# Another order of t's, s's and h's weight preparation, ahead of the loop and in its first step

## What is computed

```
kx = modulated_linear(x, cond, k...)        # 512 x 512 weights, scaled per batch by a style
A  = softmax(scores of the 16 heads of a token among themselves)   # 16 x 16 per token
x  = x + modulated_linear(A @ kx, cond, o...)

h = ln(ln(x, pw[path]), cp[comp]);  t = ln(x, tm[time]);  s = ln(x, ms[scale])
m, n, r = x + a row per batch
cat = [w0*h, w1*t, w2*m, w3*n, w4*r, w5*s]                # 6 x 512 wide
x = x + ln(silu(cat @ W1 + b1) @ W2 + b2, g, b)
```

## Time and profile before

| | us |
|---|---|
| median of three runs | 855.19 |
| lowest, highest | 854.5, 855.64 |
| the profiled execution | 856.02 |
| its span in the trace | 854.2 |

### The profile page before, as it was taken

How to read it: one execution, slowest core, us unless ns; L and a number is a source line. 1 busy time by engine, 2 the same in 40 slices (tenths; PEclk the granted TensorE clock), 3 DMA queues, 4 the chain that set the end, 5 groups by cost and what they waited for, 6 DMA issues and landing times.

```text
span 854.2 us, 19739 instructions
## 1 busy us (share of the span) xinstructions
PE 818.0 (96%) x7482; PEld 684.3 (80%) x7482; DVE 652.6 (76%) x1077; ACT 497.5 (58%) x853; POOL 588.1 (69%) x763
## 2 busy tenths in 40 slices
PE   5996888999999999999999999999999999999996
PEld 5853766888888888888888888888888888888885
DVE  3589797779887878779888778779887877778652
ACT  3595646465756647465756647565756647564531
POOL 2279659767777766777777766767777766756462
PEclk9899899999999999999999999999999999999998
DMA  8973243435544342435444342425444342333210
GB/s 279 418 259 85 63 93 75 118 66 151 107 135 113 87 106 64 118 66 152 106 138 111 87 107 62 119 67 151 108 117 104 87 110 60 106 69 82 50 51 26
DMA packets 104366, 95.56 MB, mean 112 GB/s; under 512 B 72880, under 2 KB 78160, under 8 KB 102608
## 3 DMA queue, kind: packets, MB, share of 16 engines
q1 hardware_dynamic: 95056, 69.26, 30.9%
q0 software_dynamic: 4608, 16.78, 7.2%
q10 hardware_dynamic: 4608, 8.25, 2.9%
HBM read 69.60 MB, written 8.40 MB: 91 GB/s over the span
## 4 chain that ended last, share of the span: by engine, by line
PE 84%; DVE 5%; POOL 3%; ACT 3%; DMA 2%; issue 2%; ACTq 1%; SPq 0%; DVEq 0%; POOLq 0%
PE acc L414 39%; PE tok L414 29%; PE att L414 8%; PE xp L567 6%; PE xp L414 3%; DMA kb<-in_kb 1%; POOL raw_t L1778 1%; DVE stg_e L1345 1%; POOL Wol L1701 1%; DMA BD<-q 0%; ACT junk L979 0%; ACT BD L956 0%; DVE W1sl L1336 0%; DVE W1hl L1336 0%; SPq L311 0%
## 5 line engine op out<-in xcount | busy, mean ns | idle before, releaser
L1772 POOL TENSOR_TENSOR op1l<-ytmp,op1h 128x512 f16<-128x512 f32 x64 | 81.1, 1266 | 29.0 <-ACT op1h L932 28.6
L1719 POOL TENSOR_TENSOR xlo<-xraw,xhi 128x512 fp32r<-128x512 f32 x31 | 40.7, 1313 | 56.2 <-ACT xhi L822 56.1
L414 PE MATMUL acc<-op0h,W1xh 128*128 128x256 f32 x256 | 76.1, 297 | 1.2 <-DVE op0l L1437 1.2
L414 PE MATMUL acc<-op0l,W1xh 128*128 128x256 f32 x256 | 72.4, 283 | 0.0
L414 PE MATMUL acc<-op0h,W1xl 128*128 128x256 f32 x256 | 72.3, 282 | 0.0
L414 PE MATMUL acc<-op1h,W1th 128*128 128x256 f16 x256 | 69.8, 273 | 0.0
L414 PE MATMUL acc<-op2h,W1sh 128*128 128x256 f16 x256 | 69.8, 273 | 0.0
L414 PE MATMUL acc<-op1l,W1th 128*128 128x256 f16 x256 | 69.8, 273 | 0.0
L414 PE MATMUL acc<-op1h,W1tl 128*128 128x256 f16 x256 | 69.8, 273 | 0.0
L414 PE MATMUL acc<-op2l,W1sh 128*128 128x256 f16 x256 | 69.8, 273 | 0.0
L414 PE MATMUL acc<-op2h,W1sl 128*128 128x256 f16 x256 | 69.8, 273 | 0.0
(11 more groups left out here) (287 smaller groups left out, 2815.3 us busy)
## 6 DMA issues: line engine op xcount, KB each, us to landing
xsq<-in_x SPq DMA_DIRECT2D x32, 256.0 KB, 3.1
xb<-in_x SPq DMA_DIRECT2D x32, 256.0 KB, 3.1
out<-xb SPq DMA_DIRECT2D x32, 256.0 KB, 2.3
BD<-q SPq DMA_DIRECT2D x124, 64.0 KB, 2.1
BD<-v SPq DMA_DIRECT2D x124, 64.0 KB, 3.5
xraw<-in_xT SPq DMA_DIRECT2D x30, 256.0 KB, 3.0
ring<-in_k_wT ACTq DMA_DIRECT2D x6, 256.0 KB, 3.5
dmb<-dm_rows SPq DMA_DIRECT2D x6, 256.0 KB, 4.0
```

The lines of the kernel that those rows point to most:

```text
L414: return e.matmul(o, a, b, start=start, stop=True, skip_group_check=True)
L1719: e.tensor_tensor(xlo[:, :, :], (xraw1 if g == 1 else xraw)[:, :, :], xhi[:, :, :].bitcast(F32), ALU.subtract).then_inc(s["xlo"], 1)
L1772: e.tensor_tensor(op_of[n]["l"][:, :, half(g)], four(ytmp[YT[n, g][0]]), op_of[n]["h"][:, :, half(g)], ALU.subtract).then_inc(s[f"o{n}l"], 1)
```

## The change

On GpSimd, scaled("t") moves from behind scales() to behind bounds(3), add_ob(1) moves up into its old place, and lo_16("t") moves behind gather(1) and is parted by true_scale(2). On ScalarE, z_copy(0) moves ahead of the two waits, scaled_hi("s") ahead of u_make(0), split_hi of t behind x1_hi(0), and scaled_hi("h") behind exponential(2). On VectorE, low_16("s") moves in the first step from ahead of product(pa, "h") to behind it. The numbers that are waited for on s["wh"] follow the new order (s is 1, x 2 to 5, t 6). Every instruction is still there, and the work in the steps behind the first is the same.

```diff
--- before.py
+++ after.py
@@ -1063,18 +1063,17 @@
             split_x(3)
             a_hi(1)
             squares(3)
+            z_copy(0)
             e.wait_ge(s["m2"], 3)
-            e.wait_ge(s["nst"], 8)
-            split_hi(W1["t", "h"], raw["t"], s["wh"])
-            z_copy(0)
+            scaled_hi("s")
             u_make(0)
             score_low(2)
             for kt in range(4):
                 e.wait_ge(s["xc"], kt + 3)
                 e.copy(W1["x", "h"][:, kt, :], stg["e"][:, kt, :]).then_inc(s["wh"], 1)
             x1_hi(0)
-            scaled_hi("s")
-            scaled_hi("h")
+            e.wait_ge(s["nst"], 8)
+            split_hi(W1["t", "h"], raw["t"], s["wh"])
             x1_hi(1)
             prod_hi(0, "t")
             z_make(1)
@@ -1082,6 +1081,7 @@
             e.wait_ge(s["pa"], 1)
             e.activation(t2[:, 0:256].bitcast(BF16), rp[:, :], ACT.Copy, scale=up).then_inc(s["tp"], 1)
             exponential(2)
+            scaled_hi("h")
             for k in range(1, NT + 1):
                 a, b, pa, pb = 2 * k, 2 * k + 1, 2 * k - 2, 2 * k - 1
                 front, more = k < NT, k < NT - 1
@@ -1331,7 +1331,7 @@
 
             def low_16(n, kts):
 
-                e.wait_ge(s["wh"], 6 if n == "s" else 7)
+                e.wait_ge(s["wh"], 1 if n == "s" else 7)
                 for kt in kts:
                     i = e.scalar_tensor_tensor(out=W1[n, "l"][:, kt, :], in0=raw[n][:, kt, :], scalar=beta, in1=W1[n, "h"][:, kt, :], op0=ALU.mult, op1=ALU.subtract)
                 i.then_inc(s["wlx"], 1)
@@ -1597,9 +1597,9 @@
                 product(pb, "s")
                 if front and not mod:
                     one_hot(k)
+                product(pa, "h")
                 if k == 1:
                     low_16("s", range(4))
-                product(pa, "h")
                 if mod and mod[1] == 0:
                     mod_lo(*mod, (2, 3))
                 if front:
@@ -1832,20 +1832,20 @@
             inverse_norms()
             true_scale(1)
             scales()
-            scaled("t")
+            add_ob(1)
             root1(0)
             affine(0)
             x_lo(3)
             bounds(3)
-            add_ob(1)
+            scaled("t")
             root2(0)
             add_ob(2)
-            e.wait_ge(s["wh"], 1)
-            e.wait_ge(s["Pm"], 3)
-            lo_16("t", s["wlp"])
             root1(1)
             gather(1)
+            e.wait_ge(s["wh"], 6)
+            lo_16("t", None, (0, 1))
             true_scale(2)
+            lo_16("t", s["wlp"], (2, 3))
             e.wait_ge(s["dmW"], 16)
             prod_lo(0, "t")
             for k in range(1, NT + 1):
```

## The result

| | before | after |
|---|---|---|
| median, us (runs) | 854.68 (20) | 857.07 (20) |
| lowest to highest, us | 853.06 to 857.05 | 854.24 to 859.06 |
| the profiled execution, us (its span) | 856.02 (854.2) | 858.63 (856.8) |

The ratio is 1.0023, with a 95% interval of 1.0014 to 1.0033: 2.0 us slower (1.2 to 2.8). The median before is 0.5 us under that of the three runs known ahead, so 1.9 us forecast stand against 2.0 by the ratio and 2.4 by the medians. The forecast of 857.1 met the median of 857.07, and part of that is luck: the term for x_T(1) was 1.3 us too large, and about as much more is in the runs than the traces show for any term.

A forecast was written before the change was run, and what follows sets the result against it. TensorE was taken as the bound behind the first step, VectorE's run as setting values(3); +2.7 - 0.3 - 0.6 + 0.1 = +1.9 us gave a median forecast of 857.1 us, 8-in-10 range 854.3 to 859.4.

The forecast's parts named there:

- the term for x_T(1): TensorE's x_T(1) in the first step: starts at 92.0, 2.7 us later than before, ends 1.7 and 3.5.
- The bound: Behind the first step TensorE's own work sets the end; shifts where it passes 141.53 us count one for one.
- the first part: t's scaling behind the fourth bound on GpSimd: u_make(0) 3.3 us later, x_T(1) 2.7 us later.
- the faster rival: VectorE's run to values(3) gets shorter as its 120.22 instruction meets GpSimd in another phase: -1.2 us, 854.0; chance 0.15.
- VectorE waits out the GpSimd instruction under way: VectorE instructions with two SBUF operands wait for GpSimd's to end; one x_weights of some 5 us beside the scaling.
- ScalarE's order: ScalarE's s high part is free in the wait for root2(0); h's is covered by the wait ahead of z_copy(1).
- "nothing" for t's low part: GpSimd's t low part, with true_scale(2) between, ready near 100, TensorE asking near 105: no cost.
- 0.5 for h: scaled_hi("h") ahead of z_copy(1) on ScalarE: takes back at most 0.5 us if TensorE's clock recovers sooner.
- Low part of s: VectorE's low_16("s") behind product(0,"h"): -0.6 us on the run to values(3); TensorE's 2.99 us wait moves later.
- The clock: TensorE's low clock: -0.3 us behind x_T(1) (0 to -0.8), +0.1 behind values(3) (0 to +1.3).
- The sum: All terms up to 141.53 us on TensorE: +2.7 - 0.3 - 0.6 + 0.1 = +1.9 us.
- theory C: For second traces: x_T(1) to z_T(1) on TensorE usually near 7 us before, near 8.2 with late u, by clock recovery.

The follow-up runs named there:

- With the clock kept up: The changed kernel with nine extra matmuls ahead of u_T(0) and ten ahead of x_T(1) on TensorE; 856.41 us, ratio 1.0008 to the kernel before.
- the halves: The changed kernel with scaled("t") cut in two: two kt behind scales(), two behind root2(0); 852.38 us, ratio 0.9970 to the kernel before.
- the kernel before, filled: The kernel before with ten extra matmuls, results overwritten later, in TensorE's 3.5 us wait ahead of x_T(1); 854.84 us, ratio 0.9996.

## Why the prediction was right, and where it was not

**The bound.** Right as far as the traces can tell: TensorE is as full behind scores(4) as it was, and the rest of the span varies by up to 1.9 us between traces without going with the change.

**x_T(1) later by 2.7 us: the direction was right, the size was not.** It was 1.4 (27.09 and 27.06 us behind L1797, before 25.63 twice), just under the low end of 1.7. The working has four sizes in it, and the first part is the term that was mis-sized. The bound ended 1.3 us sooner, where I counted 0.95. The scaling took 5.7 us (5.8 forecast). root2(0) took 1.7 us, not 2.2; most of the x_weights had passed by then, since the scaling held only the first of them, and not to its end. And u_make(0) to x_T(1) took 5.86 us, not 6.2, since add_ob(2) held up nothing. u_make(0) was thus 2.4 us late instead of 3.3. Two readings were off without moving this: the shortest of the four x_low ran behind lo_16("t"), not beside it, and the 1.2 us of the faster rival add up to 1.1 with its own 0.6 for product(0,"h").

**VectorE waits out the GpSimd instruction under way.** This was the step that failed in part. In all five traces with the scaling whole between bounds(3) and root2(0) the first x_weights(2) took 3.39 to 3.40 us and ended 1.2 us before the scaling did; with root2(0) ahead the last one took 4.04 us and ended 1.2 us before it too. The prediction had one x_weights of some 5 us, to the scaling's end. The lock that the Trainium skill describes ("SBUF — State Buffer", section "SBUF: two separate sides") holds for the whole instruction; here there was a wait of 2.7 us, but not to the end. On this point the measurement decides.

**ScalarE's order, and "nothing" for t's low part.** Moving h alone costs nothing that can be told. With the clock kept up a 1.12 us wait appears at values(2), as it does with the halves (1.13); the kernel before, filled, has 0.23. I had allowed 0.5 for h. But VectorE's e is 1.17 us later behind z_T(1) than in the filled kernel before, and 0.70 of that is there when the exponential starts, ahead of h: it waits for true_scale(2), for which the prediction put nothing. Only the other 0.47 us can be h's. No run moved true_scale(2) alone.

**Low part of s.** Right: -0.6 us in three pairs of traces, -1.0 by the runs (0.1 to 2.0). TensorE's 2.99 us wait went and came back at z_T(2) and values(3), as VectorE's bound demands.

**The clock: right in the traces, open in the runs.** The low clock of the first step was read too long: the granted clock is still 1.00 from 114.9 to 115.4 us and 0.50 only from 116 on, so 4.1 us should be about 3.5. I took -0.3 us up to z_T(1) and +0.1 behind values(3). In the two pairs of traces the two stretches sum to -0.1 and -0.2 us (8.22 + 8.28 against 8.38 + 8.23; 7.50 + 9.03 against 8.46 + 8.25). That is the size forecast. Over all runs, though, the changed kernel lost 1.7 us more to the low clock than the one before, so in the runs the term may well have the other sign.

**The sum.** The two traces of each kernel agree on +0.7 to +0.8 us up to scores(4), against +1.9 forecast. The runs say +2.0 (1.2 to 2.8). So 1.2 us are in the runs and not in the traces, and that they are as large as the error in the term for x_T(1) is luck. The record points at the traces of before, not at the changed kernel. Set beside them, nine of the eleven other kernels are sooner (or less late) at scores(4) than their ratios say, by 0.5 to 1.6 us; 1.1 is the median of the eleven. And both traces of before have a mean granted clock of 0.983. Of the 93 runs of before that stood beside the experiments, 23 had 0.983 or less, with a mean time of 856.0 us; the other 70 had more and a mean of 854.8. A usual run of before thus has less low clock than either trace, as the trace with low_16(s) alone has, which passes x_T(1) to z_T(1) in 7.02 us with the same lists up to there. Of the changed kernel's 20 runs 18 had 0.983 or less, so its two traces (0.983 and 0.981) are usual ones. This is worked out from sums over runs; no trace of a usual run of before was got, theory C's own test failed, and what makes the low clock end sooner in one run than in another stays open.

What is shown is where the loss hangs. With u_make(0) behind the scores and x's high parts the changed kernel is back at the time of before (0.9999), the gain from the low part of s included, though its trace is only 1.3 us sooner at scores(4); h alone costs nothing that can be told.

## What to carry to other kernels

Moving a long instruction on one engine's list moves everything behind it there, and then everything behind the waits for those on the next engine's list: moving 5.7 us of scaling made TensorE's x_T(1) 1.4 us later, 1.1 of it through the steps that stood behind u_make(0). Cutting it in two and taking root2(0) ahead of the second half, with each half where GpSimd waited anyway, was worth 4.5 us against the changed kernel. A forecast that meets the time can still have a wrong term; cut the path at points where the lists agree before calling it right. When runs differ by 4 us among themselves, one or two traces can't account for 2: look first where the traced runs stand among the others, by time and by mean granted clock. And take such a point by its instruction, not by its line number, which moves with every edit above it.

## What the runs showed of the hardware

A VectorE instruction with two SBUF operands, issued 1.1 us into a GpSimd scaling of one SBUF tensor of 128x2048, took 3.40 us instead of 0.74 and ended 1.2 us before the scaling, the same in five traces. In the other direction, the GpSimd scaling took 6.31 us whole and 3.71 for a half when it started beside two such VectorE instructions, one behind the other, 5.70 whole beside a single one, and 5.45 and 2.85 beside none. Ten extra matmuls in a 3.5 us wait kept TensorE at its higher clock (2.4 GHz; granted clock 1.00 from 88.8 to 94.8 us, 0.50 without them): from the first matmul of proj(3)'s rest to W1's first there were 2.5 us (89.53 to 92.04) instead of 4.1 (90.02 to 94.10).
